# A decoder layer's mixture-of-experts feed-forward: the short last chunk first, with centroids, gates and second biases in it, one load of weights, last products by pairs of tiles

## The reference

```python
h = relu(einsum('td,ndf->ntf', flat, shared_w1) + shared_b1[:, None, :])        # 2 shared experts
out = flat + einsum('ntf,nfd->td', h, shared_w2) + shared_b2.sum(0)
scores = sigmoid(flat @ centroids.T) + bias                                      # 16 routed experts
vals, idx = top_k(scores, 4)
gating = zeros_like(scores).at[arange(T)[:, None], idx].set(vals)
gating = gating / clip(gating.sum(-1, keepdims=True), 1e-08)
# for each routed expert j: out += (relu(flat @ w1[j] + b1[j]) @ w2[j] + b2[j]) * gating[:, j]
x = layernorm(x + (out + routed))
```

## Time and profile before

| | us |
|---|---|
| median of 3 runs (lowest, highest) | 445.69 (445.24, 446.9) |
| the profiled execution | 446.32 |
| its span, first to last instruction | 444.5 |
| TensorE busy / VectorE / ScalarE / GpSimd | 404.6 / 309.3 / 257.4 / 181.0 |
| mean granted TensorE clock | 0.976 |

### The profile page before, as it was taken

One profiled execution on the slowest core, in us unless ns is written; L12 is line 12 of the kernel. 1 busy time (PEld: TensorE's weight loads), 2 busy tenths in 40 slices (PEclk: granted clock), 3 DMA queues, 4 the chain that ended last, 5 costly groups with the idle time before them and its releaser, 6 DMA issues.

```text
span 444.5 us, 8612 instructions
## 1 busy us (share of the span) xinstructions
PE 404.6 (91%) x2609; PEld 360.2 (81%) x2609; DVE 309.3 (70%) x865; ACT 257.4 (58%) x649; POOL 181.0 (41%) x314
## 2 busy tenths in 40 slices
PE   3976998999988999889998899959999999999994
PEld 2665787999878999779997788848899988899984
DVE  1595999698988797987979866617648535644444
ACT  3457879676556676557756465614556744444442
POOL 0043656545653653655546524734846500000000
PEclk9996999999999999999999989996999999999997
DMA  7611140000000000000000600992222312342311
GB/s 216 219 49 49 55 158 2 25 1 2 0 3 24 0 0 0 0 0 0 0 0 0 190 2 4 266 252 71 74 75 93 93 53 72 88 126 96 91 47 47
DMA packets 24359, 28.28 MB, mean 64 GB/s; under 512 B 2385, under 2 KB 16874, under 8 KB 24330
## 3 DMA queue, kind: packets, MB, share of 16 engines
q1 hardware_dynamic: 24330, 27.92, 20.5%
HBM read 26.80 MB, written 1.11 MB: 63 GB/s over the span
## 4 chain that ended last, share of the span: by engine, by line
PE 67%; DVE 14%; issue 7%; SPq 4%; DMA 3%; POOL 2%; ACT 2%; DVEq 0%; POOLq 0%; ACTq 0%
PE bank L630 18%; PE bank L631 17%; PE bank L632 17%; PE bank L747 4%; PE bank L756 3%; PE bank L719 2%; PE bank L746 2%; DMA gate_rows<-gates_d 2%; DVE by_cos L1207 1%; PE bank L819 1%; DVE by_sin L1208 1%; DVE pT_lo L1096 1%; SPq L568 1%; DVE scores L1218 1%; PE bank L713 1%
## 5 line engine op out<-in xcount | busy, mean ns | idle before, releaser
L927 ACT ACTIVATE hid<-bank,b_cols 128x512 f32<-128x512 f32 (+1 forms) x50 | 34.4, 688 | 77.4 <-PE bank L632 63.7
L1109 DVE TENSOR_TENSOR hid<-hid,gate_rows 128x512 f32<-128x512 f32 (+2 forms) x46 | 32.6, 709 | 63.3 <-ACT hid L927 54.0
L1459 POOL TENSOR_SCALAR nprobs<-probs,rsums 128x128 f32<-128x128 f32 x64 | 24.2, 378 | 92.1 <-DVE rsums L1225 79.4
L631 PE MATMUL bank<-w_lo,hid_hi 128*128 128x256 f32 (+1 forms) x200 | 57.1, 286 | 0.0
L1451 POOL TENSOR_TENSOR queryT<-by_cos,by_sin 128x512 f32<-128x512 f32 x32 | 42.5, 1330 | 29.5 <-DVE by_sin L1208 28.6
L975 ACT COPY swapped<-bank 64x512 f32<-64x512 f32 x40 | 23.3, 583 | 33.4 <-PE bank L632 33.2
L1096 DVE TENSOR_TENSOR hid_lo<-hid,hid_hi 128x512 fp32r<-128x512 f32 (+1 forms) x50 | 36.8, 736 | 5.6 <-ACT hid_hi L939 5.5
L631 PEld LDWEIGHTS bank<-w_lo,hid_hi 128*128 128x128 f32 (+1 forms) x200 | 38.7, 194 | 2.0
L630 PE MATMUL bank<-xT_hi,wq_hi 128*128 128x256 f32 x128 | 38.4, 300 | 1.7 <-issue 1.2
L632 PE MATMUL bank<-x2T_hi,w_lo 128*128 128x512 f32 (+1 forms) x100 | 39.2, 392 | 0.0
L982 ACT ACTIVATE probs<-scores,ntop 128x128 f32<-128x128 f32 x64 | 25.8, 404 | 22.4 <-DVE ntop L1221 21.7
(11 more groups left out here) (174 smaller groups left out, 1293.5 us busy)
## 6 DMA issues: line engine op xcount, KB each, us to landing
gate_rows<-gates_d SPq DMA_DIRECT2D x16, 256.0 KB, 3.2
w_raw<-in_L_ffn_routed_w SPq DMA_DIRECT2D x4, 528.0 KB, 8.0
stage<-in_L_attn_q_kernel SPq DMA_DIRECT2D x4, 512.0 KB, 6.6
stage<-in_L_attn_out_kernel SPq DMA_DIRECT2D x4, 512.0 KB, 3.6
w_raw<-in_L_ffn_routed_w SPq DMA_DIRECT2D x2, 1024.0 KB, 9.6
gate_rows<-gates_d SPq DMA_DIRECT2D x8, 224.0 KB, 3.0
gate_rows<-gates_d SPq DMA_DIRECT2D x8, 192.0 KB, 2.9
gate_rows<-gates_d SPq DMA_DIRECT2D x8, 160.0 KB, 2.5
```

Source lines behind the costliest of these rows:

```text
L631: nc.tensor.matmul(o, sh, ml, start=False, stop=False, **kw)
L927: nc.scalar.activation(hid[0:n, i % 2, :], z_bank[i % 3][0:n, :], ACT.Relu, bias=b1_cols[0:n, i % NC:i % NC + 1]).then_inc(relu_done, 1)
L1109: nc.vector.tensor_tensor(hid[rows, i % 2, :], hid[rows, i % 2, :], gate_rows[rows, i % 3, :], ALU.mult).then_inc(gated, 1)
L1459: nc.gpsimd.tensor_scalar(nprobs[:, u, 0:W], probs[:, u, 0:W], rsums[:, u, 0:1], 1.0, ALU.mult, ALU.mult)
```

## The change

`TOP = 24` is the short chunk. Its matrices are widened: the first has the 16 centroids beside its 96 columns (112 in all), the second has the 16 routed and 2 shared second biases under its 96 rows (114 in all). Its hidden tile `top_hid[h]` holds 96 hidden rows, and in rows 96 to 111 first the router's logits and then, in rows 96 to 113, the transposed gates and ones.

- `up_top(h)` takes the place of `router(h)` and of the chunk's `up`; `top_out` copies the logits and makes the ReLU; `turn_logits` turns the 16 rows back to tokens. `down(24)` and `down(49)` keep their places and include the second biases; `second_biases` goes.
- The chunk is split first (`split(TOP)`, `up_low(TOP)` at the head of the lists), VectorE copies the centroids into `w1_raw` before.
- SyncE issues the top chunk's parts and then all weights before `store_gates(0)`.
- The steps other than the top chunk's are numbered by `nth_up`, buffers of `hid` and of PSUM go by it.
- The last three `down` go by pairs of tiles: tiles 4 and 5 of all three, then 6 and 7. The layer norm has three groups, tiles 0 to 3, 4 and 5, 6 and 7; tiles 6 and 7 lie in separate banks of PSUM.

```diff
             load_w1(0)
             sp.dma_start(w2_raw[:, 0:full, :], s2[0:full * P].rearrange("(n p) c -> p n c", p=P)).then_inc(ld_w[0], 16)
...
             load_w2(1, full + 1, 8)
+            load_w1(2)
+            load_w2(2, 8, 16)
+            load_w1(3)
+            load_w2(3, 16, TOP)
...
             for i in range(UNGATED, UNGATED + 3):
                 load_gates(i)
-            load_w1(2)
-            load_w2(2, 8, 16)
-            load_w1(3)
-            load_w2(3, 16, NC - 1)
-            sp.dma_start(w2_raw[0:LAST, NC - 1, :], r2[row_of(NC - 1):NR * FF]).then_inc(ld_w[3], 16)
...
+            def up_top(h):
+
+                e.wait_ge(w1_done, split_place(TOP))
+                e.wait_ge(emptied, slot_count(2 * h + 1 if h else 2, "y"))
+                if h == 1:
+                    e.wait_ge(oT_done, pv_count(B - 1, HK - 1, 1))
+                cols = slice(h * HALF, (h + 1) * HALF)
+                for k in range(KC):
+                    mm = three(top_bank[h][0:UP_COLS, :], w1_hi(TOP, k), w1_part(w1_lo, TOP, k),
+                               x2T_hi[:, k, cols], x2T_lo[:, k, cols], k == 0, k == KC - 1)
+                mm.then_inc(top_up_done, 1)
+
+            def turn_logits(h):
+                e.wait_ge(logits_out, h + 1)
+                rows = slice(LAST, LAST + NR)
                 for t in range(HT):
+                    mm = nc.tensor.transpose(logits[:, t * NR:(t + 1) * NR], top_hid[h][rows, t * P:(t + 1) * P],
+                                             ident[rows, rows])
                 mm.then_inc(routed, 1)
...
-            e.wait_ge(dve, place("dve", "centT_lo"))
             z = B - 1
             score(z, 14)
             score(z, 15)
-            router(0)
             turn(z, 11)
+            up_top(0)
             turn(z, 12)
             values(z, 2, 0)
+            turn_logits(0)
             project_out(z, 1, 1)
...
-            for i in range(NI):
-                if i + AFTER < NI:
-                    up(i + AFTER)
+            for i in range(NI - 3):
+                if not is_top(i) and nth_up(i) + AFTER < NU:
+                    up(step_of(nth_up(i) + AFTER))
                 down(i)
...
-                if i == 5:
-                    second_biases(0)
                 if i == 8:
                     slot(z, "y")
                 if i == 10:
-                    router(1)
+                    up_top(1)
+                if i == 11:
+                    turn_logits(1)
...
-                if i == NC + 5:
-                    second_biases(1)
+            for u, i in itertools.product((0, 1), range(NI - 3, NI)):
+                e.wait_ge(hid_done, i + 1)
+                down_pair(i, u)
...
+            def top_out(h):
+                e.wait_ge(top_up_done, h + 1)
+                nc.scalar.copy(top_hid[h][LAST:UP_COLS, :], top_bank[h][LAST:UP_COLS, :]).then_inc(logits_out, 1)
+                nc.scalar.activation(top_hid[h][0:LAST, :], top_bank[h][0:LAST, :], ACT.Relu,
+                                     bias=b1_cols[0:LAST, TOP:NC]).then_inc(top_relu_done, 1)
...
             z = B - 1
+            split(TOP)
             softmax_exp(z, 13)
             softmax_exp(z, 14)
-            score_exp(0)
             probs_hi(z, 11)
+            top_out(0)
             probs_hi(z, 12)
             softmax_exp(z, 15)
             heads_hi(z, 2, 0)
+            score_exp(0)
             split(0)
...
             z = B - 1
+            e.wait_ge(projected, max(slot_count(z, s) for s in SLOTS if s[0] in "xkqv"))
+            after_act("smallT")
+            nc.vector.tensor_copy(w1_raw[:, :, F:F + NR], centT[:]).then_inc(cent_placed, 1)
             mask_and_top(z, 14)
...
             z = B - 1
+            up_low(TOP)
             normalise(z, 13)
             normalise(z, 14)
             normalise(z, 15)
+            down_low(TOP)
             for c in range(6):
                 split_low(c)
```

More of the change, by code:

```diff
@@ L48 @@
 UNGATED = NS * FF // P
+TOP = NC - 1
+UP_COLS = LAST + NR
+DOWN_ROWS = LAST + NR + NS
 NI = 2 * NC
@@ L204, in rows_of, with up_cols, down_rows, is_top @@
 def rows_of(i):
-    return LAST if i % NC == NC - 1 else P
+    return LAST if i % NC == TOP else P
+def up_cols(c):
+    return UP_COLS if c == TOP else P
+def down_rows(c):
+    return DOWN_ROWS if c == TOP else P
+def is_top(i):
+    return i % NC == TOP
+def nth_up(i):
+    return i - i // NC
+def step_of(u):
+    return u + u // (NC - 1)
+NU = 2 * (NC - 1)
+def split_place(c):
+    return 1 if c == TOP else c + 2
 def gate_count(i):
@@ L480, in y_tile, with starts_bank, hid_of @@
         def y_tile(t):
[L481 to L485, removed]
+            b, half = Y_PLACE[t]
+            return bank[b][:, half * C:(half + 1) * C]
+        def starts_bank(t):
+            return Y_PLACE[t][1] == 0
+        def hid_of(i):
+            h, c = half_of(i)
+            return top_hid[h][0:DOWN_ROWS, :] if c == TOP else hid[:, nth_up(i) % 2, :]
@@ L1070, in _ @@
             split(4)
-            for i in range(2, NI):
+            for u in range(2, NU):
+                i = step_of(u)
                 relu(i)
-                if i > 2:
+                if u > 2:
+                    hid_high(step_of(u - 1))
+                if is_top(i - 1):
                     hid_high(i - 1)
-                if i + 3 < NC:
+                if i + 3 < TOP:
                     split(i + 3)
@@ L1088, in _ @@
                     final_scale(0)
+            hid_high(NI - 2)
             hid_high(NI - 1)
@@ L1156, in gate_values @@
             def gate_values(h):
-                own = gates[:, h, :, 0:NR]
+                own = gates[:, h, LAST:].rearrange("p (t r) -> p t r", r=NR + NS)[:, :, 0:NR]
                 gating_settled()
@@ L1400, in _ @@
             moments_of(z, 0)
-            for i in range(2, NI):
+            for u in range(2, NU):
+                i = step_of(u)
                 gate(i)
-                if i > 2:
+                if u > 2:
+                    hid_low(step_of(u - 1))
+                if is_top(i + 1):
+                    gate(i + 1)
+                if is_top(i - 1):
                     hid_low(i - 1)
@@ L1522, in _ @@
             keep(z, 0)
-            for c in range(13, NC):
+            for c in range(13, TOP):
                 split_low(c)
```

299 lines of the change are left out of this document (175 added, 124 removed).

## The result

The kernel after takes 425.55 us (median of 4 runs, 424.92 to 425.83), the kernel before, run beside it, 446.22 us (445.24 to 446.9): a ratio of 0.954 (95% interval 0.952 to 0.956). Forecast were 427.7 us in a range of 425.0 to 432.0. The spans of the two profiled executions are 423.6 and 444.5 us, so there are 20.9 us to place where 18.0 were forecast.

A forecast was written before the change was run, and what follows sets the result against it. TensorE, busy 91% of the span, was taken as the bound, with idleness and half clock as losses. Gains 7.8 + 2.3 + 1.7 + 1.4 + 3.8 + 1.5 - 0.5 = 18.0 us gave 427.7 us, range 425.0 to 432.0.

The forecast's parts named there:

- Step 1, one load: `up(0)` to `up(8)`: all weights issued before the gates' store end the gate-row stall; 7.8 us, 5.5 idleness and 2.3 half clock.
- 0.5 us set aside for new waits: Allowance between `up(0)` and `up(8)` for waits newly appearing once the stall goes; 0.5 us, bounds 0 and 3.
- eight products of L719: Work left on TensorE between `up(7)` and `up(8)` beside one `down`; counted at 1.99 us at full clock.
- The load's rate: 6.49 MB of weights from about 248 us at 231 GB/s, so the load ends near 276 us.
- (b): Rival: the one load is slower, 164 GB/s, so gate rows come late and TensorE stands; about 8 us back, 435.5 us; chance 0.10.
- (c): Rival: load under 130 GB/s in front of the gates, all engines stand still; 448 us and more; chance 0.03.
- Step 2, first half: End of attention: router moved inside the top chunk's `up`, so `up(0)` starts at 268.1 instead of 269.79; 1.7 us.
- rival (a): Clock falls at attention's end as before, or the added chain costs more; 1.7 to 3.5 us lost, 429.2 to 431; chance 0.18.
- Steps 2 to 4 behind `up(8)`: `up(8)` to last product: second router replaced, top chunk's old place free, second biases' products gone; 7.5 us forecast.
- Step 5, the pairs: Kernel's end: last three chunks by pairs of tiles, so tiles 4 and 5 finish early; 1.5 us gained.
- few tenths: Last three chunks: pairs need chunk 48's `hid` 0.7 us after `down(46)` instead of 1.4; a few tenths lost at worst.
- Rival (d): Kernel's end: pairs bring nothing, as three groups' norms run in series on VectorE and ScalarE; 1.5 us back, 429; chance 0.07.

## Why the prediction was right

The range held the time, and the gains lie in the five places that the prediction names. It was 2.2 us too cautious, 2.9 in the two traces, of which 0.9 is the scatter of the first line. The loads, the small products' clock and the pairs were tested by runs of their own; what the products that are gone, the top chunk's place and the second biases gained is read from the trace alone. In these terms:

- **Step 1, one load: 7.3 forecast, 8.4 measured.** The mechanism stands, by taking the step back (5.6 us lost against the kernel after), by making it alone (5.9 us gained, 6.4 to 8.5 in its stretch) and by lengthening the load (7.4 us lost). The number is that of one pair of executions: the prediction was worked out from a trace in which the stall and the clock behind it cost most, and the second pair gives 6.1. Against the first pair two terms were mis-sized. The 0.5 us set aside for new waits did not come; `w1_done`, named as what is late next, was on time. And the eight products of L719 were counted at the 1.99 us of the earlier trace rows, which is a duration and not a distance between starts: in the new trace they begin at 294.19 and the next product at 295.73, 1.54 us. The prediction had said itself that the distance is what counts in a dense run.
- **The load's rate** was taken as 231 GB/s. From 256 to 268 us it was 336 to 349 GB/s in the table by stretches, and the load was over at about 269 us instead of 276. The mean of the earlier trace rows held time in which the queue had nothing to do: by stretches of the same trace it is 5 and 34 GB/s up to 279 us and 330 to 361 from 283 to 295. It made no difference to the sum, only to the room: (b) and (c) were less likely than I had them. The Trainium skill's rule that transfers under 64 KB are dominated by their descriptors ("DMA: Bandwidth & Descriptors", the rule to batch transfers) did no harm here: the pieces of the top chunk (2 to 96 KB) took 0.28 to 0.43 us each to issue, the two of 40 KB, issued behind larger loads, took 2.60 and 1.04, their larger neighbours there 0.44 to 2.69, and the first cast that reads the top chunk's weights began at 257.23, just behind VectorE's centroid copy (256.99, 0.17 us), so it waited for the copy and not for a transfer.
- **Step 2, first half: 1.7 forecast, 1.7 measured.** The wait in front of `up_top(0)` is 0.98 us (1.3 forecast, for the same releaser, GpSimd's low part), and `values` starts at 260.69, 3.8 us behind the scores (3.9 forecast), with `up(0)` 6.5 us behind that (6.3). The 1.7 us hang on the clock: rival (a) had it falling here as before, and it did not. The prediction left open whether the small products or the idleness bring it down, and why it stayed full here isn't shown. The thinned router, with more idleness and a full clock, and the 48 small products, with no idleness and the lower clock, speak for the products; but 24 of them put back into the kernel after left the clock at 1.00 too. So that they are gone is not shown to be what kept it, and that this number came out to a tenth is in part luck. The Trainium skill ("TensorE: Matmul & The Clock Gate", "HAM oscillation") names gaps of idleness; that is seen here behind the gaps of 2.90 to 7.70 us, and is not the whole of it: 320 to 322 us in the kernel with one load alone, TensorE busy 2.00 of 2.00 us, clock 0.54.
- **Steps 2 to 4 behind `up(8)`: 7.5 forecast, 8.4 measured.** The products that are gone were worth their whole time, as the earlier trace rows had it. The surplus is the `down`'s distance, 0.023 us less over 45 of them, 1.0 us, less the 0.3 us that the pairs cost here; some 0.2 us stay without a cause. The trace of before couldn't show that distance, and the runs don't explain it.
- **The second router's clock** was in no term. In the first trace of the kernel before it does not fall there; in two later traces of kernels with that router it does, at 1.7 us each. The two executions of the kernel before still took about the same time (446.32 and 445.79 us), as the second lost 2 us less at the stall (idleness 0.8, clock behind it 1.2). In no trace of the kernel after and its variants does it fall in that place.
- **Step 5, the pairs: 1.5 forecast, 1.5 measured behind the last product.** The few tenths that the prediction allowed for at worst, and left out of its sum, were lost: 0.3 us in front of the top chunk's `down`, in every trace. So the step is worth some 1.1 us, 0.7 in the medians. Rival (d), that the pairs bring nothing, is refuted for the tail; by the times alone it isn't.

## What to carry to other kernels

A transfer that the engines wait for is as late as the bytes queued in front of it, so let large loads that can start early end before it is issued, and look at the rate of full queues, not at a mean over a stretch. Small products cost their own time and, in some executions, the clock behind them as well, so put their columns into a product that is executed anyway. Where a chain over several engines sets a stretch, moving one wait away only shows the next. And take a second trace of the same kernel before a gain is put down to a place: the kernel before lost its clock in other places from one execution to the next, and a stretch gained 8.4 us by one pair of traces and 6.1 by the other.

## What the runs showed of the hardware

- TensorE's clock went to its lower level while TensorE had no gap: at the 32nd of 48 products of 16 columns (0.11 to 0.21 us between starts at 261.8 us), and it stayed there until 272 us, 6.6 us into transposes and large products.
- Runs of 24 such products lowered it in five of eight places, in the same kernel in one execution and not in another.
- A fall of the clock cost 1.7 us in all three traces in which it came at 262 us and in both in which it came behind the second router, 2.9 and 1.7 us behind the stall in the two traces of the kernel before, and 5.1 us in and behind the 48 small products.
- The store of the gates took SyncE 0.3 us to issue on an empty queue and 5.1 us behind loads that were under way; issues of weights behind others took from 0.4 to 2.7 us in the kernel after.
- A `down` of 12 products of 256 columns took 1.436 us in all variants of the kernel before and 1.413 in all of the kernel after; the one shift of addresses that was tried did not change it.
